# Split first loads, a reordered head of VectorE's program, and the context's low parts on one engine

## The reference, cut to what matters

```python
x = x + _L0_xattn_ref(_layernorm(x), itok_BxS_13_99985, ctx_2048, ctx_2048, ctx_2048)
# in it, for e in range(4):
#   g = silu(einsum('bsd,fd->bsf', h, ctx[e])); u = einsum('bsd,fd->bsf', h, ctx[e])
#   y = einsum('bsf,df->bsd', g * u, ctx[e])
#   out = where((expert_ids == e)[..., None], y, out)     # expert_ids from the token's number
x = x + _L0_ffn_ref(_layernorm(x), ...)    # 16 routed experts, top 4, and a shared one
x = x + _L1_xattn_ref(_layernorm(x), ctx_2048, itok_BxS_0_1023, ...)
x = x + _L1_ffn_ref(_layernorm(x), ...)
```

## Time and profile before

| | us |
|---|---|
| median of 3 runs (lowest, highest) | 593.29 (591.95, 594.46) |
| the profiled execution | 591.15 |
| its span in the trace | 589.3 |
| TensorE, VectorE, ScalarE, GpSimd busy | 499.9, 449.4, 357.1, 318.0 |

### The profile page before, as it was taken

One profiled execution on the slowest core, in us unless ns is written; L12 is line 12 of the kernel. 1 busy time (PEld: TensorE's weight loads), 2 busy tenths in 40 slices (PEclk: granted clock), 3 DMA queues, 4 the chain that ended last, 5 costly groups with the idle time before them and its releaser, 6 DMA issues.

```text
span 589.3 us, 11045 instructions
## 1 busy us (share of the span) xinstructions
PE 499.9 (85%) x3338; PEld 440.2 (75%) x3338; DVE 449.4 (76%) x1358; ACT 357.1 (61%) x903; POOL 318.0 (54%) x298
## 2 busy tenths in 40 slices
PE   0599978989789998986287999999899999588894
PEld 0488757778678888985267999999899998345673
DVE  4789955964876878753778889999989887759774
ACT  2344454333547676753227887878688889666543
POOL 2547660014356887415658778788567873362200
PEclk9999998999999999996588999999899999879998
DMA  7135534323263645569501000000000000000000
GB/s 272 47 115 143 154 116 108 77 63 83 85 181 101 193 137 160 127 208 303 144 27 28 18 21 27 28 20 1 2 1 2 2 1 2 0 1 0 19 28 27
DMA packets 27816, 45.24 MB, mean 77 GB/s; under 512 B 5680, under 2 KB 18832, under 8 KB 27120
## 3 DMA queue, kind: packets, MB, share of 16 engines
q1 hardware_dynamic: 20912, 28.15, 15.5%
q0 software_dynamic: 3792, 10.74, 7.2%
q10 hardware_dynamic: 3056, 5.65, 3.0%
HBM read 34.63 MB, written 8.85 MB: 74 GB/s over the span
## 4 chain that ended last, share of the span: by engine, by line
PE 48%; DVE 22%; issue 9%; ACT 6%; DMA 6%; POOL 2%; SPq 0%; ACTq 0%; DVEq 0%; POOLq 0%
PE bank L415 8%; PE bank L416 8%; PE bank L417 8%; PE bank L1076 8%; PE bank L1516 5%; DVE X L1627 2%; PE bank L1471 1%; DVE sc L2067 1%; DMA yk<-slots_y,slot 1%; DMA bw<-bits_dram 1%; PE bank L1277 1%; PE bank L1279 1%; PE bank L1278 1%; ACT pr L952 1%; DVE pT_lo L1575 1%
## 5 line engine op out<-in xcount | busy, mean ns | idle before, releaser
L578 POOL DMA_INDIRECT inb<-rows_kept,row_of x47 | 47.0, 1000 | 37.7 <-PE bank L1076 19.5
L952 ACT ACTIVATE pr<-sc,smin 128x256 f32<-128x256 f32 x128 | 63.3, 502 | 0.0
L657 POOL TENSOR_TENSOR Q_lo<-Q,Q_hi 128x512 fp32r<-128x512 f32 x32 | 41.5, 1298 | 23.8 <-ACT Q_hi L691 23.2
L2067 DVE CUSTOM_DVE_ANT_0 sc<-bank,bias 128x256 f32<-128x256 f32 x128 | 46.5, 419 | 0.0
L1575 DVE TENSOR_TENSOR pT_lo<-bank,pT_hi 128x512 fp32r<-128x512 f32 x64 | 41.1, 683 | 4.5 <-ACT pT_hi L691 4.5
L644 POOL TENSOR_TENSOR pr<-pr,srec 128x512 f32<-128x512 f32 x32 | 33.3, 1042 | 20.7 <-DVE srec L2074 20.6
L691 ACT ACTIVATE pT_hi<-bank 128x512 fp32r<-128x512 f32 x64 | 35.0, 596 | 13.2 <-PE bank L1076 12.8
L651 POOL TENSOR_TENSOR Q<-Q,rot 128x512 f32<-128x512 f32 x32 | 41.1, 1284 | 2.0 <-DVE Q L2056 2.0
L536 POOL TENSOR_TENSOR Wd<-wd_raw,Wd 128x512 fp32r<-128x512 f32 x13 | 16.9, 1298 | 46.7 <-ACT Wd L738 46.6
L606 POOL DMA_INDIRECT yk<-slots_y,slot x32 | 33.1, 1034 | 15.2 <-issue 5.7
L415 PE MATMUL bank<-pT_hi,V_hi 128*128 128x256 f32 x128 | 36.9, 288 | 2.7 <-DVE pT_lo L1575 2.7
(11 more groups left out here) (346 smaller groups left out, 1955.7 us busy)
## 6 DMA issues: line engine op xcount, KB each, us to landing
slots_y<-yb SPq DMA_DIRECT2D x47, 128.0 KB
wg_raw<-gate_up_dram SPq DMA_DIRECT2D x22, 256.0 KB, 2.7
bw<-bits_dram ACTq DMA_DIRECT2D x3, 1024.0 KB
wd_raw<-down_dram SPq DMA_DIRECT2D x16, 128.0 KB
wo<-wo_dram SPq DMA_DIRECT2D x2, 1024.0 KB
wd_raw<-down_dram SPq DMA_DIRECT2D x30, 64.0 KB
gu_raw<-gate_up_dram SPq DMA_DIRECT2D x6, 256.0 KB, 3.3
X<-x_dram SPq DMA_DIRECT2D x2, 512.0 KB, 6.6
```

The costliest lines, as they stand in the source:

```text
L578: pool.indirect_dma_start(inb[:, j % NIN, :], None, rows_d, bass.IndirectOffsetOnAxis(row_of[:, j:j + 1], 0)).then_inc(slots_in[j % NIN], 16)
L657: pool.tensor_tensor(Q_lo[:, i % 2, :], Q[:, i % 2, :], Q_hi[:, i % 2, :].bitcast(F32), ALU.subtract).then_inc(queries_low_g, 1)
L952: e = act.activation(pr[:, i % 2, z, :], sc[:, i % 2, z, :], ACT.Exp, bias=smin[:, i % 2, z:z + 1], scale=-1.0, accum_out=ssum[:, i % 2, z ...
L2067: dve.tensor_tensor_reduce(sc[:, r, z, :], bank[2 + h][:, u * S:(u + 1) * S], bias[:, TB * b_ + u, :], 1.0, 3.0e38, ALU.add, ALU.min, smin ...
```

## The change

It touches only the start and the first passes of the loop:

- SyncE issues tile 0 of `X` alone, then the two halves (512 columns each) of the context's row 0 with `tok` between them, then tiles 1 to 3, then `seg`, then tiles 4 to 7. ScalarE issues the identity alone, then the two column halves of the context's row 1, then the rest of the table.
- The context's parts go by quarters q (column half z = q // 2, row k = q % 2): `hi_context(q)` on ScalarE and `lo_context(q)` on VectorE. GpSimd's share of it is gone. Quarter 3 is made inside pass -1.
- TensorE's first product waits for the low parts of quarters 0 and 1 before z = 0 and for 2 and 3 before z = 1.
- VectorE normalises tile 0 right after `lo_context(0)`; the masks come behind `lo_context(1)`, the moments of tiles 1 to 3 into pass -1, those of tiles 4 to 7 and the tables into pass 0 behind `gprod(0)`.
- ScalarE runs one small silu before anything else.

```diff
         def _(sp):
-            for i in range(2):
-                sp.dma_start(X[:, 4 * i:4 * i + 4, :], x_d[:, 4 * i:4 * i + 4, :]).then_inc(x_in[i], 16)
-                if i == 0:
+            def load_x(i, a, b):
+                sp.dma_start(X[:, a:b, :], x_d[:, a:b, :]).then_inc(x_in[i], 16)
+
+            load_x(0, 0, 1)
+            for z in range(2):
+                cols = slice(z * HALF, (z + 1) * HALF)
+                sp.dma_start(ctxT[:, 0, cols], ctxT_d[:, 0, cols]).then_inc(context_in[z], 16)
+                if z == 0:
                     sp.dma_start(tok[:, :], tok_d).then_inc(tokens_in, 16)
-                    sp.dma_start(seg[:, :], seg_d).then_inc(tokens_in, 16)
+            load_x(1, 1, NT // 2)
+            sp.dma_start(seg[:, :], seg_d).then_inc(tokens_in, 16)
+            load_x(2, NT // 2, NT)
...
             power(0, 0, 1).then_inc(rstd_g, 1)
-            pool.wait_ge(context_high_a, 1)
-            lo(ctx_lo[:, 0, :], ctxT[:, 0, :], ctx_hi[:, 0, :]).then_inc(context_low_g, 1)
             pool.wait_ge(variance_v, 2)
...
         def _(act):
-            act.dma_start(const[:, 0:K_COS], const_d[:, 0:K_COS]).then_inc(identity_in, 16)
-            for k in range(KD):
-                act.dma_start(ctxT[:, k, :], ctxT_d[:, k, :]).then_inc(context_in[k], 16)
+            act.dma_start(ident, const_d[:, K_ID:K_ID + P]).then_inc(identity_in, 16)
+            for z in range(2):
+                cols = slice(z * HALF, (z + 1) * HALF)
+                act.dma_start(ctxT[:, 1, cols], ctxT_d[:, 1, cols]).then_inc(context_in[z], 16)
+            act.dma_start(const[:, K_ONE:K_COS], const_d[:, K_ONE:K_COS]).then_inc(x_in[2], 16)
+            act.wait_ge(step_g, 1)
+            act.activation(fo[:, :], mhalf[:, :], ACT.Silu)
...
-            for k in range(KD):
-                act.wait_ge(context_in[k], 16)
-                copy(ctx_hi[:, k, :], ctxT[:, k, :]).then_inc(context_high_a, 1)
-
+            def hi_context(q):
+
+                z, k = divmod(q, 2)
+                act.wait_ge(context_in[z], 32)
+                copy(ctx_hi[:, k, z * HALF:(z + 1) * HALF], ctxT[:, k, z * HALF:(z + 1) * HALF]).then_inc(context_high_a, 1)
+
+            for q in range(3):
+                hi_context(q)
...
                     hi1(i + 1)
+                if i == -1:
+                    hi_context(3)
...
                 for z in range(2):
+                    if t == 0:
+                        pe.wait_ge(context_low_v, KD * (z + 1))
...
             for i in range(-1, NT + 5):
-                if i == 0:
-                    pe.wait_ge(context_high_a, KD)
-                    pe.wait_ge(context_low_v, 1)
-                    pe.wait_ge(context_low_g, 1)
...
+            def lo_context(q):
+
+                z, k = divmod(q, 2)
+                cols = slice(z * HALF, (z + 1) * HALF)
+                dve.wait_ge(context_high_a, q + 1)
+                lo(ctx_lo[:, k, cols], ctxT[:, k, cols], ctx_hi[:, k, cols]).then_inc(context_low_v, 1)
...
+            lo_context(0)
             norm1(0)
-            for t in range(1, NT // 2):
-                moments(0, t)
-            dve.tensor_scalar(vare[:, 0, 1:NT // 2], mv[:, 0, 1:NT // 2, 1], EPS, None, ALU.add).then_inc(variance_v, 1)
-            dve.wait_ge(context_high_a, 2)
-            lo(ctx_lo[:, 1, :], ctxT[:, 1, :], ctx_hi[:, 1, :]).then_inc(context_low_v, 1)
+            lo_context(1)
+            expert_masks()
+            lo_context(2)
             for i in range(-1, NT + 5):
...
                     lo1(i + 1)
+                if i == -1:
+                    lo_context(3)
+                    dve.wait_ge(x_in[1], 16)
+                    for t in range(1, NT // 2):
+                        moments(0, t)
+                    dve.tensor_scalar(vare[:, 0, 1:NT // 2], mv[:, 0, 1:NT // 2, 1], EPS, None, ALU.add
+                                      ).then_inc(variance_v, 1)
...
                     gprod(i)
-                if i == -1:
-                    dve.wait_ge(x_in[1], 16)
+                if i == 0:
+                    dve.wait_ge(x_in[2], 32)
                     for t in range(NT // 2, NT):
                         moments(0, t)
                     dve.tensor_scalar(vare[:, 0, NT // 2:NT], mv[:, 0, NT // 2:NT, 1], EPS, None, ALU.add
                                       ).then_inc(variance_v, 1)
+                    tables()
```

More of the change, by code:

```diff
@@ L248, in build @@
             m[k] for k in "lanes hit pt comb lane tileno row_f tile_p".split()]
-        x_in = [sem(f"x_in{i}") for i in range(2)]
+        x_in = [sem(f"x_in{i}") for i in range(3)]
         context_in = [sem(f"context_in{i}") for i in range(KD)]
@@ L266, in build @@
          gated_low_v, experts2_p, x_after1_v, norm_turned_p, norm_high_a, norm_low_v, routed_p, context_high_a,
-         context_low_v, context_low_g, identity_in, step_g, stats_v, router_high_a,
+         context_low_v, identity_in, step_g, stats_v, router_high_a,
          router_low_v, small_in, kv_kept, egu_high_a, egu_low_g, edn_high_a, edn_low_g, edn_low_v) = [sem(n) for n in (
@@ L271, in build @@
              "experts2_p x_after1_v norm_turned_p norm_high_a norm_low_v routed_p context_high_a context_low_v "
-             "context_low_g identity_in step_g stats_v router_high_a router_low_v small_in "
+             "identity_in step_g stats_v router_high_a router_low_v small_in "
              "kv_kept egu_high_a egu_low_g edn_high_a edn_low_g edn_low_v").split()]
@@ L1591, in _ @@
             dve.tensor_scalar(vare[:, 0, 0:1], mv[:, 0, 0, 1:2], EPS, None, ALU.add).then_inc(variance_v, 1)
[L1592 to L1605, removed]
@@ L1606, in _, with expert_masks @@
-            copy(one16[:, :], ones)
+            def expert_masks():
+                dve.wait_ge(tokens_in, 32)
+                for e_ in range(3):
+                    link(dve.tensor_scalar(ge[:, e_, :], tok[:, :], float((e_ + 1) * PER_EXPERT), None, ALU.is_ge))
+                dve.tensor_scalar(pick[:, 0, :], ge[:, 0, :], -1.0, 1.0, ALU.mult, ALU.add)
+                dve.tensor_tensor(pick[:, 1, :], ge[:, 0, :], ge[:, 1, :], ALU.subtract)
+                dve.tensor_tensor(pick[:, 2, :], ge[:, 1, :], ge[:, 2, :], ALU.subtract)
+                copy(pick[:, 3, :], ge[:, 2, :])
+                copy(segf[:, 0, :], seg[:, :])
+                link(dve.tensor_scalar(segf[:, 1, :], seg[:, :], float(-LOOKBACK), None, ALU.add))
@@ new lines, in tables @@
+            def tables():
+                link(dve.tensor_tensor(hn[:, 2, 0:P], ident, keyix[:, 0:P], ALU.mult))
+                link(dve.tensor_reduce(rowix[:, :], hn[:, 2, 0:P], AX_X, ALU.add))
+                dve.tensor_scalar(upper[:, :], rowix[:, :], float(R), None, ALU.is_ge)
+                dve.tensor_scalar(tri[:, :], keyix[:, 0:P], rowix[:, 0:1], None, ALU.is_gt)
+                copy(one16[:, :], ones)
+            def lo_context(q):
[3 more added lines that the diff above has]
+                lo(ctx_lo[:, k, cols], ctxT[:, k, cols], ctx_hi[:, k, cols]).then_inc(context_low_v, 1)
```

## The result

The changed kernel is slower: 593.82 us median of 20 runs, the kernel before 587.89 over 20 runs. The ratio on record is 1.0075 (95% interval 1.0055 to 1.0096), which is 4.4 us. The two medians by themselves lie 5.9 us apart (1.0101), above that interval, so the size of the step is less sure than the interval says. The kernel before came out 5.4 us lower here than in the three runs that the prediction had, so its absolute 595.1 was met partly by luck, and the step is what has to be explained: +1.8 forecast, +4.4 measured. The profiled execution took 594.82, span 593.0.

A forecast was written before the change was run, and what follows sets the result against it. The prediction took a TensorE and VectorE chain as the bound, its loop start set by the variance of tiles 4 to 7. Later variance 0.6 plus lost clock 1.2 gave +1.8 on 593.29: 595.1 us, range 591.8 to 597.8.

The forecast's parts named there:

- The anchor: Loop start: V, not the first product, sets when the loop gets going, through GpSimd's low parts and weight loads.
- V: End of the variance of tiles 4 to 7, which GpSimd's power awaits; forecast at 21.15 against 20.52 us.
- Rival 2: Start's gain is kept: the first 5.9 us come through because gT_hi(0) does not hang on V; 587.4 us, chance 0.1.
- The clock's fall: TensorE's clock drops in a wait of over 8 us before the third product, slowing the matmuls behind it.
- rival 3: Slower for real: seg lands at 10 us, V 1.9 later, twelve slow matmuls; +4.3 us, 597.6 us, chance 0.2.
- V: +0.6 forecast: Moments of tiles 4 to 7 now behind gprod(0): V is first matmul + 10.05, 0.6 us later.
- the estimate that the prediction put beside its sum: Loads at start, by the skill's bandwidth table: seg lands near 10.5 us and the sum is about +3.6.
- Clock: +1.2 forecast: Third product: eight slow matmuls cost 1.6 us, less 0.38 that VectorE may not feel, so 1.2 us.
- the 0.38 of TensorE's nearness: gT_hi of the third pass waits 0.38 us for TensorE's work; VectorE may not feel that much TensorE lateness.
- the bound of 2.4: Third product, upper bound of the clock term: all twelve matmuls slow and all felt by VectorE, 2.4 us.
- same 0.61 and slower 0.28: Whole kernel: chance 0.61 of a change within 0.5% (3.0 us), 0.28 of slower beyond it.
- the prediction's first premise: Chain of waits over TensorE and VectorE: a shift of the first passes shifts the end by as much.

The follow-up runs named there:

- e1: Changed kernel with the moments and variances of tiles 4 to 7 moved back from pass 0 to pass -1; ratio 0.9983 against the kernel before.
- e4: Changed kernel plus 36 useless matmuls in TensorE's wait ahead of the third product; ratio 1.0019 against the kernel before.
- e5: Changed kernel with the seg transfer taken out of the wait ahead of the expert masks; ratio 1.0027 against the kernel before.
- e8: Changed kernel with the loads of the kernel before, engine orders as changed; ratio 1.0123 against the kernel before.
- e10: Changed kernel without the early silu, so the table load returns to the first real silu; one run, first gT_lo 30.21 us.
- e2: Changed kernel with GpSimd's third power moved behind the low parts of the first two expert-weight pieces; ratio 0.9944 against the kernel before.
- e3: Kernel before with only GpSimd's third power moved behind the first two weight pieces' low parts; ratio 0.9974 against the kernel before.
- e6: Changed kernel with GpSimd's third power behind two weight pieces, seg out of the masks' wait, 14 useless matmuls; ratio 0.9910 against the kernel before.
- e7: Changed kernel with GpSimd's third power later, seg out of the masks' wait, 10 useless matmuls, tables in pass 1; ratio 0.9948 against the kernel before.
- e9: Changed kernel with GpSimd's third power behind two weight pieces and seg out of the masks' wait, no useless matmuls; ratio 0.9924 against the kernel before.

## Why the prediction was right

**The anchor held.** The prediction said that V, not the first product, sets when the loop gets going. From V to the first `gT_lo` are 7.35 us in the kernel before, 7.34 changed, 7.51, 7.47, 7.45, 7.39 and 7.54 in e1, e4, e5, e8 and e10, over a range of V from 18.9 to 24.8. So the third and fourth weight pieces came at 27.25 and 28.64 instead of 26 and 27.5, as V was 1.1 later than forecast. Only where GpSimd's order was changed is it another: 1.86 (e2), 5.99 (e3), 1.87 (e6), 0.83 (e7) and 1.86 (e9). Rival 2, the start's gain kept, is refuted: 5.2 us were won at the first matmul and none came through.

**The clock's fall held**, 0.50 behind a wait of 9.16 us ("over 8" was forecast), and e4_busy_tensor shows it as a cost. The rule of the Trainium skill that the prediction cited ("TensorE: Matmul & The Clock Gate", section "HAM oscillation — how this bites in real kernels"), that waits between bursts throttle TensorE again, agrees with it.

**Both terms were too small; their sizes are near those of rival 3.** What failed are the sizes of the two terms, not the mechanism:

- *V: +0.6 forecast, +1.71 measured.* `seg` landed at 9.57 instead of 8.7 (the estimate that the prediction put beside its sum had 10.5), and the first matmul came at 11.87 instead of 11.1. The prediction let the transfer land a little after the bytes ahead of it. The volume was right (234 GB/s x 8.3 us = 1.94 MB), the order was not: the context's second half, with 1.25 MB issued up to its end, was expected by 7.3 and released ScalarE only at 8.42, so part of the 1.94 MB belonged to transfers issued behind it. From first matmul to V are 10.36 instead of 10.05, as ten of the first twelve matmuls were slow, not eight. Those last 0.31 need not be the change's: the way from first matmul to V is 10.23 in e5_seg_apart with nine slow matmuls and 10.72 in e4_busy_tensor with twelve.

```profile
0.00:8.30 8.30, 0.66 (x2) 0.29 (x2) 2.38 (x6) 2.64 (x4) 0.85 (x6) 1.00 0.75 234
```

- *Clock: +1.2 forecast, +2.46 measured* (4.17 - 1.71). All twelve matmuls were slow, where I had taken the eight of the first product, and VectorE felt all of it: the 0.38 of TensorE's nearness was no slack. That is the bound of 2.4 that the prediction gave, and e4_busy_tensor, with V where it was, took 2.66 of the third `gT_lo` back.

Together the head comes out at +4.17 us in the trace; the timed runs say +4.4 by the ratio and +5.9 by the medians. With all parts of the sum at their upper bounds, rival 3 had +4.3. So the forecast named the right road with the wrong weights: same 0.61 and slower 0.28 should have stood nearer to the reverse. Luck had its part in the range too. As a step from its own 593.29, the range 591.8 to 597.8 reaches from -1.5 to +4.5, and +4.4 lies just inside; laid from the 587.89 of the 20 runs it would end at 592.4, and 593.82 lies outside. I had taken about the middle of each bound. That both terms came out high has no common cause that the runs show: e5_seg_apart took 1.6 off the first, and from V to the third `gT_lo` are 20.98 there and 20.95 in the changed kernel.

**What stays open.** The shift of the third `gT_lo` explains the ratios (table) to about 0.3%, but for e2_gpsimd_first, where it leaves 0.5% open: 0.49 us earlier at the third `gT_lo`, 3.3 us faster by the ratio. Behind the head, single profiles wander: against the kernel before, the changed one is +4.1 at 80 us, +3.0 at 104, +2.4 at 182, +4.9 at 208, +3.2 at 580 and +3.7 in the whole span, and e5_seg_apart, 2.6 later at the head, was 3.0 earlier by 323. The steps lie at 80 to 104 us, between 170 and 300, and between 500 and 549, where no edit touched the program. I ran nothing to find their cause, so that the prediction's first premise, that a shift of the head shifts the end by as much, is shown for the ratios as a group and not for a single profile.

## What to carry to other kernels

Before moving work "behind" something, ask who waits for that work on any engine and what is queued behind that waiter: here a moment of tiles 4 to 7 held a power on GpSimd, that held two low parts, these held two buffers, and these a load for which ScalarE stood still in front of the critical copy. A start made earlier only lengthens the idle time ahead of such a link, and on TensorE the longer wait costs clock besides. Cut the link first; then an earlier start is worth something, though not its full amount here. With GpSimd's order changed in both, the changed kernel (e2) began its first product 5.1 us ahead of the kernel before (e3); at the first `gT_lo` 2.8 of them were left, and at the third none, as TensorE's clock had fallen in e2. With `seg` apart and TensorE kept busy as well (e6), 7.2 us at the first product became 4.7 and 3.9.

## What the runs showed of the hardware

- TensorE's clock fell behind a short wait too. In e9_two_edits the last wait before the third product was 2.12 us; in the stretch of 3.9 us before the product TensorE was busy 1.85, and the granted clock behind it was 0.51. In the kernel before the wait was longer, 2.68 us, and all of the product behind it ran at 1.00, its matmuls 0.23 apart. So the length of the last wait alone doesn't tell. In e1_moments_back, behind a wait of 1.84 us, the clock was up when the third product began and fell during it, 0.87 in the first stretch and 0.65 in the next, with TensorE busy throughout:

```profile
27.60:28.50 0.90, 0.87 (x3) 0.87 0.71 257
28.50:33.00 4.50, 4.50 (x17) 0.65 0.43 113
```

- A transfer of 4 KB (`seg`) landed 6.5 us after its issue, and to take it out of a wait was worth about 1.5 us at the first matmul. The four kernels with that edit have it at 10.04 to 10.80, the four with the same loads and without it at 11.52 to 12.13.
